# Moving the last projections of a narrow layer by one step, and 128 unused bytes in front of one tile

## The reference

```python
# wide (layers 0, 2)
q, k, v = hidden @ Wq, enc @ Wk, enc @ Wv
logits = einsum('bhqd,bhkd->bhqk', q, k) * scale + col_bias
out = einsum('bhqk,bhkd->bhqd', softmax(logits), v)
out = out.reshape(B, HW, HEADS * HEAD_DIM) @ Wo + bo + hidden
# narrow (layers 1, 3)
xn = rmsnorm(x, norm_w)
q, k, v = xn @ wq, cond @ wk, cond @ wv
attn = softmax(einsum('btgrd,bsgd->bgrts', q, k) * scale)
out = x + einsum('bgrts,bsgd->btgrd', attn, v).reshape(B, T, 512) @ wo
```

## Time and profile before

| | us |
|---|---|
| median of 3 runs (2031.94 to 2032.82) | 2032.44 |
| the profiled execution, its own time | 2031.63 |
| its span, first to last instruction | 2029.8 |
| PE busy in the span | 1998.7 |
| DVE busy | 1434.8 |
| ACT busy | 986.0 |
| POOL busy | 646.8 |

### The profile page before, as it was taken

How to read it: one execution, slowest core, us unless ns; L and a number is a source line. 1 busy time by engine, 2 the same in 40 slices (tenths; PEclk the granted TensorE clock), 3 DMA queues, 4 the chain that set the end, 5 groups by cost and what they waited for, 6 DMA issues and landing times.

```text
span 2029.8 us, 31330 instructions
## 1 busy us (share of the span) xinstructions
PE 1998.7 (98%) x11482; PEld 1739.3 (86%) x11482; DVE 1434.8 (71%) x2488; ACT 986.0 (49%) x1814; POOL 646.8 (32%) x518
## 2 busy tenths in 40 slices
PE   8999999999999999999999989999999999999998
PEld 8999988888888887888888878888888878888887
DVE  4423367767777767888888667777767677888886
ACT  3222355445544455555554544544445555555553
POOL 0000043222222254554443432222222354444441
PEclk9999999999999999999999999999999999999999
DMA  8789742222222223343333322222222232333322
GB/s 233 152 172 210 189 90 62 78 62 61 69 78 71 65 65 99 103 120 95 93 89 92 86 85 72 72 67 77 62 62 67 77 92 72 99 95 84 89 74 85
DMA packets 262538, 191.02 MB, mean 94 GB/s; under 512 B 197522, under 2 KB 199986, under 8 KB 259826
## 3 DMA queue, kind: packets, MB, share of 16 engines
q1 hardware_dynamic: 262386, 189.03, 36.3%
HBM read 132.66 MB, written 56.26 MB: 93 GB/s over the span
## 4 chain that ended last, share of the span: by engine, by line
PE 49%; issue 32%; POOL 13%; DVE 4%; ACT 1%; SPq 0%; DMA 0%; POOLq 0%; DVEq 0%; ACTq 0%
POOL prob L1404 6%; PE acc_bank L899 6%; PE ctx_bank L270 4%; PE t_bank L877 4%; PE ctx_bank L271 4%; PE ctx_bank L272 4%; POOL x_s L1379 4%; PE acc_bank L270 3%; PE q_bank L855 3%; PE q_bank L857 3%; PE q_bank L859 3%; PE acc_bank L272 3%; PE acc_bank L271 3%; POOL rest L1413 2%; PE s_bank L270 2%
## 5 line engine op out<-in xcount | busy, mean ns | idle before, releaser
L1404 POOL TENSOR_TENSOR prob<-prob,rinv 128x1232 f32<-128x1232 f32 x128 | 288.5, 2254 | 1014.4 <-DVE rinv L1254 1014.4
L855 PE MATMUL q_bank<-x_s,w_s 128*128 128x512 f32 x768 | 316.2, 412 | 0.8 <-POOL w_s L1397 0.8
L859 PE MATMUL q_bank<-x_s,w_s 128*128 128x512 f32 x768 | 307.8, 401 | 0.0
L270 PE MATMUL acc_bank<-o_s,w_s 128*128 128x512 f32 x752 | 305.5, 406 | 2.2 <-DVE o_s L1245 2.2
L857 PE MATMUL q_bank<-x_s,w_s 128*128 128x512 f32 x768 | 307.1, 400 | 0.0
L272 PE MATMUL acc_bank<-o_s,w_s 128*128 128x512 f32 x752 | 294.6, 392 | 0.0
L271 PE MATMUL acc_bank<-o_s,w_s 128*128 128x512 f32 x752 | 293.1, 390 | 0.0
L1068 ACT ACTIVATE s_bank<-bias_s 128x308 f32<-128x308 f32 x256 | 109.8, 430 | 368.3 <-DVE prob L1216 368.3
L899 PE MATMUL acc_bank<-pT_s,vals_s 128*128 128x512 f32 x1024 | 282.1, 395 | 5.5 <-DVE pT_s L1231 5.5
L1212 DVE TENSOR_REDUCE mx<-s_bank 128x4 f32<-128x308 f32 x512 | 241.7, 472 | 60.4 <-PE s_bank L272 49.9
L1083 ACT ACTIVATE prob<-prob,rstd 128x308 f32<-128x308 f32 x256 | 141.3, 553 | 280.9 <-DVE prob L1216 252.0
(11 more groups left out here) (107 smaller groups left out, 4142.2 us busy)
## 6 DMA issues: line engine op xcount, KB each, us to landing
stream<-x_back SPq DMA_DIRECT2D x128, 256.0 KB, 2.7
x_front<-stream SPq DMA_DIRECT2D x96, 256.0 KB, 3.4
x_back<-stream SPq DMA_DIRECT2D x96, 256.0 KB, 3.7
kvw_raw<-kvw SPq DMA_DIRECT2D x17, 1024.0 KB, 8.5
k_scr<-k_out SPq DMA_DIRECT2D x36, 308.0 KB, 9.3
keys_s<-k_scr SPq DMA_DIRECT2D x128, 77.0 KB, 2.4
v_scr<-v_out SPq DMA_DIRECT2D x8, 1024.0 KB
vals_s<-v_scr SPq DMA_DIRECT2D x512, 6.5 KB
```

The lines of the kernel that those rows point to most:

```text
L270: pe.matmul(out, weights[0], moving[0], start=start, stop=False)
L855: pe.matmul(out, w[0], x_now[0], start=k == 0, stop=False)
L859: mm = pe.matmul(out, w[1], x_now[0], start=False, stop=k == XC - 1)
L1404: pool.tensor_tensor(view, view, rinv[:, slot].unsqueeze(2).broadcast_to([P, TILES * GH, CTX]), ALU.mult).then_inc(p_norm, 1)
```

## The change

For the last batch of layer 1 (`gb` = 15) the four projections m = 0, 1, 2, 3 went to steps 65, 66, 67, 67. With `m // 2` they go to steps 65, 65, 66, 66. The last batch of layer 3 is not in this table (a separate function `finish` computes it), so nothing changes there. The second edit puts a tile of 128 bytes, which nothing uses, ahead of `pT_s`; `pT_s`, `x_back` and `stage` begin 128 bytes later.

```diff
@@ Plan.projections
                     else:
-                        at = GROUPS * gb + 5 + (m if b < B - 1 or layer == 3 else (0, 1, 2, 2)[m])
+                        at = GROUPS * gb + 5 + (m if b < B - 1 else m // 2)
                     if at == s:
                         found.append((gb, m, h))
@@ whole_block
         q_s = sb("q_s", [P, 2, 2, 2, TOK], F32R)
         prob = sb("prob", [P, 2, TILES, SC], F32)
+        sb("gap", [P, 32], F32)
         pT_s = sb("pT_s", [P, 6, TOK], F32R)
```

## The result

The changed kernel takes 2020.38 us, the median of 4 runs (2020.28 to 2021.21). The kernel before, beside it on the same chip, takes 2032.19 (2030.86 to 2032.82, 4 runs). The ratio is 0.9944 with a 95% interval of 0.9926 to 0.9961: 11.8 us less.

A forecast was written before the change was run, and what follows sets the result against it. PE was taken to bound the kernel, busy 1998.7 of 2029.8 us. Steps 65 to 68 at 17.61 + 16.52 + 11.38 + 18.42 = 63.93 for 72.17, gap 0: 2032.44 - 8.24 = 2024.2 us, range 2021.8 to 2028.1.

The forecast's parts named there:

- What bounds the kernel: Whole kernel: PE's matmuls plus its few standstills set the time, and a change of order can only earn the standstills.
- Steps 65 to 68: Last batch of layer 1: 63.93 us in place of 72.17, that is -8.24 us.
- The softmax stall: Step 68: paid once, 1.90 us above a clean step; rival of a larger stall in step 66 or 68, chance 0.09.
- The wait of 7.85 us on ACT: Before the `woA1` copy: waits for projection (15, 3), goes with 4.02 and 1.72 us; rival, transfer came last, chance 0.06.
- Third quarter of `woA1`: Step 68: lands at latest 12.6 us in, ACT asks at 10.8 and waits up to 1.8; taken as 0.
- The transfers: Stores from `x_back` at its new address: hidden, 0 us; rival of exposed stores, at 0.16 us each +12.2, chance 0.01.
- The gap: 128 bytes ahead of `pT_s`: no effect of where a tile starts, 0 us; rival, slower by its place, chance 0.03.
- the term of the 1024 matmuls L899: Matmuls that read `pT_s`, 395 ns each: 0 us, bounds -5.1 and +5.1 from groups at 390 and 400 ns.
- the neighbouring case of the table: Rival of more gain: DVE has the step-68 stall covered, another 1.90 us goes, 2022.3 us; chance 0.06.
- A sign that the prediction had named for being wrong: Outside steps 65 to 68: the prediction is wrong if mean durations there move; no size given.

The follow-up runs named there:

- the later weights: Against the kernel before, only the load and copies of `woA1` moved one step later, projections and tiles unchanged; 2025.74 us, ratio 0.9971.
- all0: Changed kernel with 16 more unused bytes ahead of `vals_s`, so that all these tiles start at a multiple of 256; 2029.84 us, ratio 0.9991 to the kernel before.
- the bench: Separate kernels of 48-matmul stretches at chosen tile places, 27 with PE alone or beside writers, then 54 with PE alone; 226.7 to 236.5 ns with PE alone.

## Why the prediction was wrong, and where it was right

**What bounds the kernel: right.** What the table removed was PE's idle time in steps 65 to 68 and the clock behind it; PE is now at 99% of the span. The gap earned its part elsewhere: PE never stood still in the 25 steps, its matmuls themselves follow each other faster.

**Steps 65 to 68: right, each within 0.15 us.** 17.59 (17.61 forecast), 16.52 (16.52), 11.30 (11.38), 18.28 (18.42), as shown above. The positions read from layer 0 carried over. The softmax stall is paid in step 68 as forecast, L900 waiting 0.86 us where step 4 had 0.98. The wait of 7.85 us on ACT was the projection's. In the kernel before, SP issued the two quarters that ACT then waited to copy at 1163.95 us, in step 66:

```profile
1163.95 0.84 SPq L744 DMA_DIRECT2D stage<-woA  x2
```

With 3.9 us to land they were there by about 1168, some 13 us before ACT began to wait (1188.66 - 7.85 = 1180.81). So the transfer wasn't what it waited for, and the wait ends with the table alone and with the later weights, which both bring the projection ahead of the copies.

**Third quarter of `woA1`: right.** It is there 10.9 us into step 68, ACT waits 0.17 us for it, of a bound of 1.8, and the bias for step 69 is not late.

**The transfers: right at nothing.** The stores take 2.7 us to land before and after:

```profile
stream<-x_back SPq DMA_DIRECT2D x128, 256.0 KB, 2.7
```

The gap one tile later, which gives `x_back` and `stage` their new addresses and moves nothing else, changes the time by -0.2 us, within its interval. By the rule of the Trainium skill, DMA: Bandwidth & Descriptors, section How a descriptor splits into AXI transactions, a DMA descriptor that doesn't start at a multiple of 256 bytes costs extra beats. No run here shows it: the median landing is 2.74 us with `x_back` at 112, 2.72 at 240, and 2.73 in `all0`, where it starts at a multiple of 256.

**The gap: the step that failed.** The prediction put it as "I see no effect of where a tile starts" and sized the term of the 1024 matmuls L899 at 0, between -5.1 and +5.1 us. It is 1024 x (229.1 - 231.7) ns = -2.7 us by their distances, and -2.5 us in the time of the gap alone. Two things were wrong in the reading. It compared the mean durations of three groups of matmuls, and durations of overlapping matmuls don't show their spacing: that of L858 stays at 400 ns while the distance from L856 to L858 falls by 1.2 ns. And it let one comparison on each side cancel, though the groups differ in all their tiles at once, so that neither comparison says what moving one tile does. The bound of 5.1 us was then left out of the range, which reached down only to the neighbouring case of the table, 2022.3. With the bound taken in, the range would have reached 2019.1 and held the result. A sign that the prediction had named for being wrong did come, that mean durations outside steps 65 to 68 move: 393 ns for 395.

**The whole difference.** The predicted span was 2021.6 us and it is 2018.5. Of the 3.1 us, 0.24 lie in steps 65 to 68, 2.33 in the rest of the pipeline, where the gap acts, and 0.53 ahead of the first scores, where both kernels run the same code: I take that part for chance between executions.

**Shown and open.** Shown: the gap acts through the place of `pT_s` within 256 bytes together with those of other tiles (a move by 256, or of all tiles by 128, undoes it); it is in PE's spacing, at full clock and without any wait, and nearly all behind the matmuls that read `pT_s`; in the bench PE's own tiles give such differences and the writers tried beside it none. Open: which tiles act together beyond the half that `vals_s` carries, and by what mechanism. The bench's order of places isn't the kernel's: with PE alone, moving at 0 on stationary at 0 was among the shortest patterns (226.7 ns), but `o_s` at 0 on `w_s` at 0 made the kernel 13 us slower. The kernel mixes matmuls of four shapes, and the bench has one.

## What to carry to other kernels

When a queue's engine waits for the bound engine's last work of a step, and that engine's next step needs what stands behind the wait, count the ring as a whole: the wait, the clock behind it, and the late softmax; a position of the same list of work elsewhere in the program gave its cost to 0.15 us here. In a kernel that PE bounds, changing a tile's size or order can move the matmuls by parts of a per cent, as it did here: compare a long stretch of identical work before and after, separate that from the edit by a version with the addresses alone, and put such a term's bound into the range. Don't look for a rule such as "align everything"; try a few paddings and measure.

## What the runs showed of the hardware

- The start-to-start distance of 128x512 matmuls at full clock depends on where the tiles start within 256 bytes: 226.7 to 236.5 ns with PE alone. 16 unused bytes ahead of `o_s` cost 25 wide steps 416.65 - 412.74 = 3.9 us and the kernel 13.
- Moving all tiles by 128 bytes left it as it was in the kernel (413.40 us) and from 0 to 128 in the bench (226.7 ns), but equal places aren't alike: both tiles at 16 have 230.1 ns and at 112 233.3.
- Identical matmuls on identical places ran at 231.0 or 226.7 ns in one execution, with different stretches ahead of them.
- DVE, ACT and POOL writing tiles of 128x512 beside PE, all three at once, left the distance at 226.7 ns with PE's tiles at 0.
- For kernels with the same places, or with all of them moved by 128, the length of 413 us of such work repeats to 0.01 us, so a difference of 27 ns in a step can be read from single executions.
